# Attention stages of a four-layer decoder: output turned ahead of the weights, context keys ahead of the first turn, the addition and its norm one step later

## The chip, the cores and the metric

The kernel runs on one core of one Trainium2 chip. The time is that of the device, in microseconds (us), for one launch that does the whole decoder; lower is better. The core has five engines that run beside each other and meet at semaphores: TensorE (PE, with its weight loads PEld), VectorE (DVE), ScalarE (ACT), GpSimd (POOL) and SyncE (SP), which issues the transfers.

## What is computed

A decoder of four layers on 32 sequences of 64 tokens of 128 features, in float32. Each layer has a self-attention, an attention to a context and a feed-forward part, each with a residual addition. Six of the twelve parts go through the function that is changed. Cut to what matters, with one of the six written out:

```python
x = x + L0_attn(_layernorm(x), ...)                 # L0a: relative bias added to the scores
x = x + L1_xattn(_layernorm(x), ctx_1024, ...)      # L1x: plain softmax, keys and values of the context
x = x + L2_attn(_layernorm(x), ...)                 # L2a: low-rank maps, norms of queries and keys, causal
x = x + L3_attn(_layernorm(x), ...)                 # L3a: scores times a table of distances, causal
x = x + L3_xattn(_layernorm(x), ctx_1024, ...)      # L3x: sparsemax in place of softmax
x = x + L3_ffn(_layernorm(x), ...)                  # L3f: holds an attention (causal), then a gated part

def _L3_attn_ref(x, Wq, Wk, Wv, Wo, bo, rel_emb):
    q, k, v = heads(x @ Wq), heads(x @ Wk), heads(x @ Wv)        # 16 heads of 8
    scores = jnp.einsum('bhqd,bhkd->bhqk', q, k) * a_k
    scores = jnp.where(causal, -jnp.inf, scores)
    attn = jax.nn.softmax(scores / np.sqrt(hd), axis=-1)
    ctx = jnp.einsum('bhqk,bhkd->bhqd', attn, v)
    return merge(ctx) @ Wo + bo
```

## The kernel before, in words

The 2048 tokens are 16 tiles of 128 tokens (two sequences each), and four tiles make a quarter. A stage is one block with a program for each engine, written out in order; between stages all engines meet. Inside a stage the order of work is that in which the loops of `attention` (line 474) are written, and semaphores alone hold an engine back.

All engines run a loop over steps k of the same kind, one new tile a step, with later phases of earlier tiles behind it. `lag` is 1 in L0a and L3x and 2 in the others (line 527). On TensorE a step k is (lines 649 to 674): `scores(k)`, `turn_probs(k-lag)` (8 transposes of the weights), `turn_output(k-lag-2)` (a transpose of the normalised output), `weigh_values(k-lag-1)` (32 short matmuls in the trace, 16 in the program), `project(k-lag-2)`; in steps 1 and 2 of a quarter the keys and queries, and the values, of the quarter ahead follow. On VectorE a step k is (lines 940 to 955): `shift(k)` (two to four instructions over 128x1024), `normalise(k-lag-1)`, `add(k-lag-2)` of the projected tile to x, `measure` of the same tile, `scale(k-lag-3)`. ScalarE takes the transposed weights out of PSUM (two copies), then the transposed output, then makes the exponentials of tile k; in the sparse stage L3x the last (a Relu) comes first in the step. GpSimd spreads the keys of tile k over the heads (line 833) and inverts the variance for the norm of a later tile (line 842).

Outputs, turned outputs and projected tiles of tile t lie in PSUM bank 4 + t % 2 (lines 519 to 521). So `weigh_values(t)` may write only when `add(t-2)` has read the bank, and it waits for that:

```python
if t >= 2:
    pe.wait_ge(s.y_added, t - 1)
```

`scores(t)` waits until the scores of tile t-1 are read: after the first VectorE instruction of `shift` in L0a and L2a and L3f, after the second in L3a (semaphore `scored`), after the last in L1x (`shifted`). L3x computes all its scores ahead of the loop and runs twice, on 8 tiles each time; its VectorE step begins with `less_threshold(k)` in place of `shift(k)`. In L3f the addition goes to h and no norm follows inside the stage.

In the semaphore lists below, of stage L0a, signal_0_9 is `scores_ps`, 0_11 `scored`, 0_14 `probs_ready`, 0_15 `probsT_ps`, 0_16 `probsT_ready`, 0_17 `o_ps`, 0_19 `att_ready`, 0_21 `oT_ready`, 0_22 `y_ps` and 0_23 `y_added`.

Of the kernel before, what the change touches and what calls it, by code (L numbers as in the profile page):

```python
# [13 lines left out]
ACT = mybir.ActivationFunctionType  # L14
# [459 lines left out]
def attention(c, n, keys_from="h", mode="plain", q_scale=1.0, exp_scale=1.0, bias=False,  # L474
# [53 lines left out]
    with nc.Block() as block:  # L528
        @block.tensor
        def _(pe):  # L530
            def turn(q):
# [5 lines left out]
                    last = pe.transpose(c.ps[:, 6, tok(t % HT)], src[:, t], c.w("ident"))  # L537
                last.then_inc(s.turned_ps, 1)

            def keys_and_queries(q):  # L540
                pe.wait_ge(s.turned, q + 1)
                if q > 0:
                    pe.wait_ge(s.vx_ready, values_taken(q))
                pe.matmul(c.ps[:, 7], c.w(n + "_wk"), kvT[:, quarter(q)], start=True, stop=True).then_inc(s.k_ps, 1)
                pe.matmul(c.ps[:, 6], c.w(n + "_wq"), c.hT[:, quarter(q)], start=True, stop=True).then_inc(s.q_ps, 1)

            def values_of(t):
# [75 lines left out]
            def project(t):  # L623
                pe.wait_ge(s.oT_ready, t + 1)
                if out_bias:
                    pe.matmul(y_ps(t), c.w("ones")[0:1], c.w(n + "_bo")[0:1], start=True, stop=False)
                pe.matmul(y_ps(t), c.oT[:, tok(t)], c.w(n + "_wo"), start=not out_bias, stop=True)\
                    .then_inc(s.y_ps, 1)

            turn(0)  # L630
            if latent:
                for t in tiles_of(0):
# [16 lines left out]
            for k in range(nt + lag + 2):  # L649
                ahead, step = k // HT + 1, k % HT  # L650
                if not sparse:
                    if k < nt:
                        scores(k)
                    if k == 0 and not latent:
                        values(0)
                    if ahead < quarters and step == 0:
                        turn(ahead)
                if 0 <= k - lag < nt:
                    turn_probs(k - lag)
                if 0 <= k - lag - 2 < nt:  # L660
                    turn_output(k - lag - 2)
                if 0 <= k - lag - 1 < nt:
                    weigh_values(k - lag - 1)
                if 0 <= k - lag - 2 < nt:
                    project(k - lag - 2)
                if ahead < quarters and not sparse:
                    if latent and step < 2:
                        for t in range(HT * ahead + 2 * step, HT * ahead + 2 * step + 2):
                            latent_maps(t)
                    if latent and step == 3:  # L670
                        latent_turn(ahead)
                    if not latent and step == 1:
                        keys_and_queries(ahead)
                    if not latent and step == 2:
                        values(ahead)

        @block.scalar
        def _(act):
# [58 lines left out]
            def weights(k):  # L737
                if sparse:
                    act.wait_ge(sp.less_tau, k + 1)
                else:  # L740
                    act.wait_ge(s.shifted, k + 1)
                act.activation(buf(k), buf(k), ACT.Relu if sparse else ACT.Exp,  # L742
                               scale=exp_scale).then_inc(s.probs_ready, 1)

            take_turned(0)
            if latent:
                for t in tiles_of(0):
                    take_maps(t)
                take_roots(0)
                take_queries(0)  # L750
                take_keys(0)
            else:
                take_keys(0)
                take_queries(0)
            if sparse:
                for t in range(nt):
# [8 lines left out]

            for k in range(nt + lag + 2):
                ahead, step = k // HT + 1, k % HT
                if k < nt and sparse:
                    weights(k)
                if not sparse:  # L770
                    if k == 0 and not latent:
                        take_values(0)
                    if ahead < quarters and step == 0:
                        take_turned(ahead)
                t = k - lag
                if 0 <= t < nt:
                    for j in range(2):
                        act.wait_ge(s.probsT_ps, 2 * t + j + 1)
                        if t >= 2:

                            act.wait_ge(s.o_ps, t - 1)
                        act.copy(probsT(t)[:, j * 512:(j + 1) * 512], c.ps[:, 2 + j])\  # L782
                            .then_inc(s.probsT_ready, 1)
                t = k - lag - 2
                if 0 <= t < nt:
                    act.wait_ge(s.oT_ps, t + 1)
                    if bias:

                        act.activation(c.oT[:, tok(t)], oT_ps(t), ACT.Identity, bias=c.w(n + "_bv"))\
                            .then_inc(s.oT_ready, 1)  # L790
                    else:
                        act.copy(c.oT[:, tok(t)], oT_ps(t)).then_inc(s.oT_ready, 1)
                if k < nt and not sparse:
                    weights(k)
                if ahead < quarters and not sparse:
                    if latent and step < 2:
                        for t in range(HT * ahead + 2 * step, HT * ahead + 2 * step + 2):
                            take_maps(t)
                    if latent and step == 2:
                        take_roots(ahead)  # L800
                    if latent and step == 3:
                        take_queries(ahead)
                        take_keys(ahead)
                    if not latent and step == 1:
                        take_keys(ahead)
                        take_queries(ahead)
                    if not latent and step == 2:
                        take_values(ahead)

        @block.gpsimd  # L810
        def _(g):
            c.begin(g)
            if bias:
                g.tensor_scalar(c.scaled_bias[:], c.w(n + "_bq"), q_scale, None, ALU.mult)\
                    .then_inc(s.bias_scaled, 1)
            if rms:
                for q in range(2):
                    norm_gpsimd(c, g, r, 1e-6, q, "rms")
            if sparse:
                row_starts = c.room(6)[:, 0:nt * HEADS * TOP]  # L820
                g.memset(row_starts, 1.0).then_inc(sp.row_starts, 1)
                g.wait_ge(sp.row_starts, 1)
                g.memset(row_starts.rearrange("p (r k) -> p r k", k=TOP)[:, :, 0], 0.0)\
                    .then_inc(sp.row_starts, 1)

            def spread_keys(t):

                g.wait_ge(s.keys_ready, t + 1)
                if t >= 2:

                    g.wait_ge(s.scores_ps, t - 1)
                of_tile = c.room(2)[:, in_ring(t)].rearrange("p (b k) -> p b k", b=2)
                g.tensor_tensor(kx(t).rearrange("p (b h k) -> p b h k", b=2, k=S), bcast(of_tile, 2, HEADS // 2),  # L833
                                bcast(bcast(c.w("head_of_row"), 2, S), 1, 2), ALU.mult)\
                    .then_inc(s.kx_ready, 1)

            behind = nt if sparse else lag + 3
            for k in range(nt + behind):
                if k < nt:
                    spread_keys(k)  # L840
                if not rms and 0 <= k - behind < nt:
                    invert(c, g, following, k - behind)
                if rms and k % HT == 2 and k // HT + 2 < quarters:
                    norm_gpsimd(c, g, r, 1e-6, k // HT + 2, "rms")

        @block.vector
        def _(v):
# [89 lines left out]
                latent_norms(0)  # L937
            if sparse:
                thresholds(c, v, s, sp, buf)
            for k in range(nt + lag + 3):  # L940
                ahead, step = k // HT + 1, k % HT
                if k < nt:
                    if sparse:
                        less_threshold(k)
                    else:
                        shift(k)
                if 0 <= k - lag - 1 < nt:
                    normalise(k - lag - 1)
                if 0 <= k - lag - 2 < nt:
                    add(k - lag - 2)  # L950
                    if not rms:
                        v.wait_ge(s.y_added, k - lag - 1)
                        measure(v, following, c.x, k - lag - 2)
                if not rms and 0 <= k - lag - 3 < nt:
                    scale(v, following, c.x, c.h, k - lag - 3)
                if latent and ahead < quarters:
                    if step in (1, 2):
                        for t in range(HT * ahead + 2 * step - 2, HT * ahead + 2 * step):
                            latent_sums(t)
                    if step == 2:  # L960
                        latent_means(ahead)
                    if step == 3:
                        latent_norms(ahead)
                if rms and ahead + 1 < quarters:
                    if step == 2:
                        norm_measure(c, v, r, c.h, ahead + 1)
                    if step == 3:
                        norm_scale(c, v, r, c.h, c.hn, ahead + 1, "rms", c.w(n + "_n1"))
# [1409 lines left out]
```

## Time and profile before

| | |
|---|---|
| time, median of 3 runs | 2032.86 us (2019.84 to 2037.69) |
| profiled execution | 2030.96 us, its span 2029.1 us |
| mean granted TensorE clock of it | 0.762 of full |
| PE busy | 1271.8 us, 63% |
| DVE busy | 1104.3 us, 54% |
| POOL busy | 660.4 us, 33% |
| ACT busy | 556.2 us, 27% |

The changed function runs from about 125 to 229 us (L0a), 798 to 883 (L1x), 996 to 1160 (L2a), 1548 to 1669 (L3a), 1669 to 1867 (L3x, twice) and 1870 to 1979 (L3f). The rest of the span is other stages. A start of a step is best seen at the 128x1024 instructions of VectorE, which come once a tile. In a timeline an instruction's end is its start plus its duration; a number in square brackets is idle time of the engine just before, and the instruction that ended it.

### The profile page before, as it was taken

To read this page: it belongs to the slowest core of one execution; us is meant where nothing else is said; L and a number is where in the kernel's file an instruction comes from. 1 tells how busy PE (TensorE), PEld (TensorE's weight loads), DVE (VectorE), ACT (ScalarE), POOL (GpSimd) and SP (SyncE) were. 2 spreads that over 40 slices of the span, in tenths; PEclk is the share of its full clock that TensorE was granted. 3 is DMA by queue.
4 is the path that set the end of the run, shared out by engine and by line. 5 is a ranking of instruction groups with operands and counts; after the bars stand their busy time and mean duration, and the time that the engine had idled before them with its cause. 6 is when DMAs were issued, how large, how long until landed. Compare 5 with 4: busy or idle time off the path is not lost. (4 is left out here: it accounts for less than half of the span.)

```text
span 2029.1 us, 34354 instructions
## 1 busy us (share of the span) xinstructions
PE 1271.8 (63%) x13592; PEld 975.5 (48%) x13592; DVE 1104.3 (54%) x2991; ACT 556.2 (27%) x983; POOL 660.4 (33%) x697
## 2 busy tenths in 40 slices
PE   3049441883888886965366734338773874747797
PEld 3026341772677774644234524226661552525465
DVE  2039861114688885872467665612326965354673
ACT  0025210330122223621155211011112423332443
POOL 1015625332234443534222210542223322323321
PEclk7569655996899997967677665569996876655788
DMA  9970002552000000002000001024421000000000
GB/s 285 178 111 2 1 5 85 156 170 73 1 2 2 2 2 1 2 6 89 30 1 1 18 5 22 17 98 132 134 94 40 1 1 1 1 1 1 1 2 22
DMA packets 74052, 91.11 MB, mean 45 GB/s; under 512 B 5823, under 2 KB 61186, under 8 KB 73248
## 3 DMA queue, kind: packets, MB, share of 16 engines
q1 hardware_dynamic: 67872, 78.95, 15.7%
q0 software_dynamic: 6016, 9.93, 1.4%
q8 instruction: 108, 1.77, 0.3%
q14 instruction: 56, 0.46, 0.1%
HBM read 58.62 MB, written 32.69 MB: 45 GB/s over the span
## 5 line engine op out<-in xcount | busy, mean ns | idle before, releaser
L833 POOL TENSOR_TENSOR arena<-arena,small 128x1024 f32<-128x1024 f32 x96 | 184.4, 1927 | 160.8 <-ACT arena L691 98.5
L386 POOL TENSOR_SCALAR var_eps<-moments 128x1 f32<-128x1 f32 (+1 forms) x136 | 43.1, 317 | 415.3 <-DVE moments L379 415.3
L593 PE MATMUL ps<-arena,q 64*64 64x512 f32 x768 | 125.6, 727 | 59.8 <-issue 20.8
L742 ACT ACTIVATE arena<-arena 128x1024 f32<-128x1024 f32 x92 | 97.3, 1058 | 183.6 <-DVE arena L907 133.8
L603 PEld LDWEIGHTS ps<-small,arena 128*128 128x128 f32 x736 | 99.0, 164 | 81.4 <-ACT arena L742 47.0
L603 PE MATMUL ps<-small,arena 128*128 128x128 f32 x736 | 120.5, 317 | 24.5 <-ACT arena L742 22.7
L615 PE MATMUL ps<-vx,arena 128*64 128x18 f32 x3072 | 128.2, 230 | 0.7 <-DVE x L921 0.7
L615 PEld LDWEIGHTS ps<-vx,arena 128*64 128x64 f32 x3072 | 118.3, 162 | 20.9 <-issue 15.9
L1680 PEld LDWEIGHTS ps<-hT,L_qkv 128*128 128x128 f32 x1024 | 120.6, 197 | 14.2 <-DVE arena L1819 13.0
L1804 POOL TENSOR_TENSOR arena<-arena 128x1024 f32<-128x1024 f32 x32 | 75.4, 2357 | 158.2 <-DVE arena L1819 158.2
L1680 PE MATMUL ps<-hT,L_qkv 128*128 128x128 f32 x1024 | 125.4, 282 | 0.7 <-ACT hT L1765 0.7
L537 PE MATMUL ps<-small,h 128*128 128x128 f32 x80 | 17.7, 361 | 163.6 <-PEq L2217 97.8
L782 ACT COPY arena<-ps 128x512 f32<-128x512 f32 x192 | 104.2, 587 | 52.7 <-PE ps L603 52.0
L1350 PEld LDWEIGHTS ps<-expert_ring,arena 128*128 128x128 f32 (+1 forms) x864 | 105.2, 193 | 5.0 <-DVE arena L1572 1.9
L1331 PE MATMUL ps<-arena,expert_ring 128*112 128x256 f32 x368 | 86.4, 389 | 32.8 <-DVE arena L1572 30.2
L1350 PE MATMUL ps<-expert_ring,arena 128*128 128x128 f32 (+1 forms) x864 | 105.5, 276 | 1.7 <-DVE arena L1572 1.7
L388 POOL TENSOR_TENSOR rstd<-var_eps,minus_half 128x1 f32<-128x1 f32 (+1 forms) x136 | 94.9, 698 | 11.3
L537 PEld LDWEIGHTS ps<-small,h 128*128 128x128 f32 x80 | 11.5, 182 | 175.9 <-issue 175.4
L1586 DVE COPY arena<-ps 128x256 f32<-128x256 f32 x31 | 13.2, 425 | 142.2 <-PE ps L1350 142.2
L1331 PEld LDWEIGHTS ps<-arena,expert_ring 128*112 128x112 f32 x368 | 64.4, 180 | 50.9 <-issue 34.8
L1436 POOL DMA_INDIRECT home_L2f<-arena,home x46 | 44.8, 973 | 131.3 <-DVE arena L1586 102.9
L1339 PE MATMUL ps<-arena,expert_ring 128*128 128x256 f32 x248 | 66.4, 414 | 25.3 <-DMA expert_ring<-L0f_in 14.5
(324 smaller groups left out, 2811.0 us busy)
## 6 DMA issues: line engine op xcount, KB each, us to landing
expert_ring<-L2f_in SPq DMA_DIRECT2D x23, 704.0 KB, 4.3
expert_ring<-L0f_in SPq DMA_DIRECT2D x23, 578.0 KB, 3.9
slots_L0f<-blank SPq DMA_DIRECT2D x1, 8385.0 KB, 74.8
slots_L2f<-blank SPq DMA_DIRECT2D x1, 8385.0 KB, 58.4
small<-small_in SPq DMA_DIRECT2D x1, 4199.5 KB, 19.5
expert_ring<-L1f_in SPq DMA_DIRECT2D x8, 512.0 KB
arena<-slots_L0f SPq DMA_DIRECT2D x23, 129.0 KB, 3.2
arena<-slots_L2f SPq DMA_DIRECT2D x23, 129.0 KB
```

The lines of the kernel that those rows point to most:

```text
L388: g.tensor_tensor(m.rstd_of[:, own], m.var_eps_of[:, own], c.minus_half[:, 0:n], ALU.pow).then_inc(m.rstd, 1)
L593: last = pe.matmul(c.ps[part(b), m], c.q[part(m), at:at + S], kx(t)[part(m), b * 512:(b + 1) * 512], start=True, stop=True)
L603: last = pe.transpose(c.ps[:, 2 + k, j * P:(j + 1) * P], buf(t)[:, (4 * k + j) * P:(4 * k + j + 1) * P], c.w("ident"))
L615: last = pe.matmul(o_ps(t)[part(b), j * 18:(j + 1) * 18], probsT(t)[:, seq(j, b)], c.vx[:, t % 8, b, j], start=True, stop=True)
L742: act.activation(buf(k), buf(k), ACT.Relu if sparse else ACT.Exp, scale=exp_scale).then_inc(s.probs_ready, 1)
L782: act.copy(probsT(t)[:, j * 512:(j + 1) * 512], c.ps[:, 2 + j])\
L833: g.tensor_tensor(kx(t).rearrange("p (b h k) -> p b h k", b=2, k=S), bcast(of_tile, 2, HEADS // 2), bcast(bcast(c.w("head_of_row"), 2, S), ...
L1331: last = pe.matmul(c.ps[0:width, 2 * (m % 2) + k, cols], ring(j)[:, k * hid + i * width:k * hid + (i + 1) * width], xT(j), start=True, sto ...
L1339: last = pe.matmul(c.ps[:, m % 4, cols], ring(j)[:, i * P:(i + 1) * P], xT(j), start=True, stop=True)
L1350: last = pe.matmul(c.ps[:, 4 + j % 2, tok(b)], hidden(j)[:, i, tok(b)], ring(j)[0:width, down_at + i * D:down_at + (i + 1) * D], start=(i ...
L1680: last = pe.matmul(c.ps[:, pair(t, i) + m, (j % 4) * P:(j % 4 + 1) * P], w[:, at:at + P], c.hT[:, tok(t)], start=True, stop=True)
L1804: g.tensor_tensor(rotated[i], rotated[i], sines[i], ALU.add).then_inc(signal, 1)
```

## The change

In `attention`, on all engines:

- TensorE: `turn_output(k-lag-2)` goes ahead of `turn_probs(k-lag)`. Where the keys come from the context (L1x, L3x) the keys of quarter 0 are projected ahead of the first turn.
- ScalarE: the copy of the turned output goes ahead of the two copies of the turned weights; the context keys are taken first; in L3x the Relu of tile k goes to the end of the step.
- VectorE: `add` handles tile k-lag-3 in step k instead of k-lag-2, and stands between `shift(k)` and `normalise(k-lag-1)`; `measure` (same tile as `add`) stays behind `normalise`, `scale` handles k-lag-4. The loop is one step longer.
- GpSimd: the inversion comes one step later.

No instruction is added or removed, and no wait is changed. The diff, cut to its core:

```diff
             def keys_and_queries(q):
                 pe.wait_ge(s.turned, q + 1)
                 if q > 0:
                     pe.wait_ge(s.vx_ready, values_taken(q))
-                pe.matmul(c.ps[:, 7], c.w(n + "_wk"), kvT[:, quarter(q)], start=True, stop=True).then_inc(s.k_ps, 1)
+                if q > 0 or keys_from == "h":
+                    project_keys(q)
...
+            if keys_from == "ctx":
+                project_keys(0)
             turn(0)
...
+                if 0 <= k - lag - 2 < nt:
+                    turn_output(k - lag - 2)
                 if 0 <= k - lag < nt:
                     turn_probs(k - lag)
-                if 0 <= k - lag - 2 < nt:
-                    turn_output(k - lag - 2)
                 if 0 <= k - lag - 1 < nt:
                     weigh_values(k - lag - 1)
...
-                if k < nt and sparse:
-                    weights(k)
...
+                t = k - lag - 2
+                if 0 <= t < nt:
+                    act.wait_ge(s.oT_ps, t + 1)
...
+                        act.copy(c.oT[:, tok(t)], oT_ps(t)).then_inc(s.oT_ready, 1)
                 t = k - lag
...
-                if k < nt and not sparse:
+                if k < nt:
                     weights(k)
...
-            behind = nt if sparse else lag + 3
+            behind = nt if sparse else lag + 4
...
-            for k in range(nt + lag + 3):
+            for k in range(nt + lag + 4):
                 ahead, step = k // HT + 1, k % HT
                 if k < nt:
                     if sparse:
                         less_threshold(k)
                     else:
                         shift(k)
+                if 0 <= k - lag - 3 < nt:
+                    add(k - lag - 3)
                 if 0 <= k - lag - 1 < nt:
                     normalise(k - lag - 1)
-                if 0 <= k - lag - 2 < nt:
-                    add(k - lag - 2)
-                    if not rms:
-                        v.wait_ge(s.y_added, k - lag - 1)
-                        measure(v, following, c.x, k - lag - 2)
                 if not rms and 0 <= k - lag - 3 < nt:
-                    scale(v, following, c.x, c.h, k - lag - 3)
+                    v.wait_ge(s.y_added, k - lag - 2)
+                    measure(v, following, c.x, k - lag - 3)
+                if not rms and 0 <= k - lag - 4 < nt:
+                    scale(v, following, c.x, c.h, k - lag - 4)
```

The first place is TensorE in L0a, from the scores of one tile (L593, now L597) to the projection (L626/L627, now L630/L631). Before:

```order
L593 MATMUL ps<-arena,q 64x512 [waits signal_0_11,signal_0_8,signal_0_5]
L593 MATMUL ps<-arena,q 64x512 x3
L603 MATMUL ps<-small,arena 128x128 [waits signal_0_16,signal_0_14]
L603 MATMUL ps<-small,arena 128x128 x3
L603 MATMUL ps<-small,arena 128x128 [waits signal_0_16]
L603 MATMUL ps<-small,arena 128x128 x3
L621 MATMUL ps<-small,att 128x128 [waits signal_0_19]
L615 MATMUL ps<-vx,arena 64x18 [waits signal_0_16,signal_0_7,signal_0_23]
L615 MATMUL ps<-vx,arena 64x18 x15
L626 MATMUL ps<-small 128x128 [waits signal_0_21]
```

And now:

```order
L597 MATMUL ps<-arena,q 64x512 [waits signal_0_11,signal_0_8,signal_0_5]
L597 MATMUL ps<-arena,q 64x512 x3
L625 MATMUL ps<-small,att 128x128 [waits signal_0_19]
L607 MATMUL ps<-small,arena 128x128 [waits signal_0_16,signal_0_14]
L607 MATMUL ps<-small,arena 128x128 x3
L607 MATMUL ps<-small,arena 128x128 [waits signal_0_16]
L607 MATMUL ps<-small,arena 128x128 x3
L619 MATMUL ps<-vx,arena 64x18 [waits signal_0_16,signal_0_7,signal_0_23]
L619 MATMUL ps<-vx,arena 64x18 x15
L630 MATMUL ps<-small 128x128 [waits signal_0_21]
```

The transpose of the output (L621, now L625) has moved ahead of the eight transposes of the weights (L603, now L607); the weighing (L615, now L619) waits for `y_added` (signal_0_23) as it did.

The second place is VectorE in L0a, one step from the first instruction of `shift` to the scaling. Before:

```order
L894 TENSOR_TENSOR arena<-ps,bias 128x1024 [waits signal_0_9,signal_0_15]
L905 TENSOR_REDUCE row_max<-arena 128x16 [waits signal_0_11]
L907 TENSOR_TENSOR arena<-arena,row_max 128x1024 [waits signal_0_12]
L913 RECIPROCAL row_inv<-ps 128x16 [waits signal_0_17]
L915 TENSOR_TENSOR att<-ps,row_inv 128x128 [waits signal_0_18]
L921 TENSOR_TENSOR x<-x,ps 128x128 [waits signal_0_22]
L376 BN_STATS stats<-x 128x6 [waits signal_0_23]
L379 BN_AGGR moments<-stats 128x2 [waits signal_0_25]
L395 TENSOR_SCALAR h<-x,moments,rstd 128x128 [waits signal_0_28]
```

And now:

```order
L901 TENSOR_TENSOR arena<-ps,bias 128x1024 [waits signal_0_9,signal_0_15]
L912 TENSOR_REDUCE row_max<-arena 128x16 [waits signal_0_11]
L914 TENSOR_TENSOR arena<-arena,row_max 128x1024 [waits signal_0_12]
L928 TENSOR_TENSOR x<-x,ps 128x128 [waits signal_0_22]
L920 RECIPROCAL row_inv<-ps 128x16 [waits signal_0_17]
L922 TENSOR_TENSOR att<-ps,row_inv 128x128 [waits signal_0_18]
L376 BN_STATS stats<-x 128x6 [waits signal_0_23]
L379 BN_AGGR moments<-stats 128x2 [waits signal_0_25]
L395 TENSOR_SCALAR h<-x,moments,rstd 128x128 [waits signal_0_28]
```

The addition (L921, now L928) has moved from behind the normalising (L913 and L915, now L920 and L922) to ahead of it, and is that of the tile before.

The third place is ScalarE in the first part of L3x, the steps of its last two tiles (these two lie in the expert ring). L742 (now L748) is the Relu, L782 (now L798) the two copies of the turned weights, L789 (now L787) the turned output. Before:

```order
L742 ACTIVATE expert_ring<-expert_ring 128x1024 [waits signal_1_42]
L782 COPY arena<-ps 128x512 [waits signal_1_17,signal_1_15] x2
L789 ACTIVATE oT<-ps,small 128x128 [waits signal_1_20]
L742 ACTIVATE expert_ring<-expert_ring 128x1024 [waits signal_1_42]
L782 COPY arena<-ps 128x512 [waits signal_1_17,signal_1_15] x2
L789 ACTIVATE oT<-ps,small 128x128 [waits signal_1_20]
```

And now:

```order
L748 ACTIVATE expert_ring<-expert_ring 128x1024 [waits signal_1_42]
L787 ACTIVATE oT<-ps,small 128x128 [waits signal_1_20]
L798 COPY arena<-ps 128x512 [waits signal_1_17,signal_1_15] x2
L748 ACTIVATE expert_ring<-expert_ring 128x1024 [waits signal_1_42]
L787 ACTIVATE oT<-ps,small 128x128 [waits signal_1_20]
L798 COPY arena<-ps 128x512 [waits signal_1_17,signal_1_15] x2
```

The order within a step was Relu, weights, output, and is now output, weights, Relu.

## Rows read from the trace of the kernel before

**Rows 1.** Page, part 1: busy us (share of the span) x instructions.

```profile
PE 1271.8 (63%) x13592; PEld 975.5 (48%) x13592; DVE 1104.3 (54%) x2991; ACT 556.2 (27%) x983; POOL 660.4 (33%) x697
```

**Rows 2.** Windows: columns from:to, us, engines busy, PEclk, DMA, GB/s; L0a, L1x, L3a, L3x, L3f.

```profile
130.00:213.00 83.00, 73.00 (x914) 47.67 (x913) 74.05 (x121) 45.80 (x76) 39.55 (x40) 0.96 0.02 5
798.00:871.00 73.00, 67.97 (x841) 42.80 (x840) 53.34 (x99) 43.85 (x75) 38.87 (x38) 0.93 0.01 2
1556.00:1651.00 95.00, 77.24 (x854) 50.19 (x848) 91.20 (x131) 42.17 (x73) 36.89 (x37) 0.89 0.00 1
1716.00:1766.00 50.00, 37.00 (x360) 31.32 (x360) 21.81 (x57) 18.82 (x32) 9.71 (x16) 0.60 0.00 1
1878.00:1967.00 89.00, 72.60 (x849) 47.31 (x845) 70.86 (x110) 42.47 (x73) 30.05 (x23) 0.83 0.00 1
```

**Rows 3.** Timeline, DVE, L0a: start us, us, instruction [idle before <-releaser].

```profile
204.77 1.22 DVE L894 TENSOR_TENSOR arena<-ps,bias 128x1024 f32<-128x1024 f32 x1
...
208.47 0.24 DVE L913 RECIPROCAL row_inv<-ps 128x16 f32<-128x16 f32 x1
...
208.95 0.28 DVE L921 TENSOR_TENSOR x<-x,ps 128x128 f32<-128x128 f32 x1
...
209.92 1.22 DVE L894 TENSOR_TENSOR arena<-ps,bias 128x1024 f32<-128x1024 f32 x1
```

**Rows 4.** Timeline, PE, same step of L0a.

```profile
205.67 1.11 PE L615 MATMUL ps<-vx,arena 128*64 128x18 f32 x32
206.71 0.48 PE L626 MATMUL ps<-small 1*128 1x128 f32 x2
207.13 0.49 PE L627 MATMUL ps<-small,oT 128*128 128x128 f32 x2
207.56 1.09 PE L593 MATMUL ps<-arena,q 64*64 64x512 f32 x8
```

**Rows 5.** Timeline, all engines, L0a where DVE waits for scores.

```profile
182.01 1.02 PE L545 MATMUL ps<-hT,small 128*128 128x512 f32 x2
...
182.96 1.09 PE L593 MATMUL ps<-arena,q 64*64 64x512 f32 x8
...
184.19 1.23 DVE L894 TENSOR_TENSOR arena<-ps,bias 128x1024 f32<-128x1024 f32 x1 [0.48 <-PE ps L593]
```

**Rows 6.** Timeline, all engines, last tiles of L0a.

```profile
216.91 1.90 PE L615 MATMUL ps<-vx,arena 128*64 128x18 f32 x32
...
218.74 0.79 PE L626 MATMUL ps<-small 1*128 1x128 f32 x2
...
219.46 0.80 PE L627 MATMUL ps<-small,oT 128*128 128x128 f32 x2
...
220.05 0.42 PE L621 MATMUL ps<-small,att 128*128 128x128 f32 x1
220.30 0.29 DVE L921 TENSOR_TENSOR x<-x,ps 128x128 f32<-128x128 f32 x1 [0.85 <-PE ps L627]
...
220.64 0.62 PE L615 MATMUL ps<-vx,arena 128*64 128x18 f32 x8 [0.17 <-DVE x L921]
```

**Rows 7.** Timeline, all engines, L2a, scores after an idle stretch.

```profile
1124.81 1.99 PE L593 MATMUL ps<-arena,q 64*64 64x512 f32 x8 [2.75 <-issue]
...
1126.93 1.23 DVE L900 TENSOR_TENSOR arena<-ps,small 128x1024 f32<-128x1024 f32 x1 [6.03 <-PE ps L593]
```

**Rows 8.** Timeline, all engines, one step of L3x, first part.

```profile
1735.76 1.22 DVE L925 TENSOR_TENSOR arena<-arena,row_inv 128x1024 f32<-128x1024 f32 x1
...
1738.91 0.38 ACT L789 ACTIVATE oT<-ps,small 128x128 f32<-128x128 f32 x1
...
1739.35 0.79 PE L626 MATMUL ps<-small 1*128 1x128 f32 x2 [0.86 <-ACT oT L789]
...
1740.90 0.29 DVE L921 TENSOR_TENSOR x<-x,ps 128x128 f32<-128x128 f32 x1 [1.78 <-PE ps L627]
...
1741.88 1.22 DVE L925 TENSOR_TENSOR expert_ring<-expert_ring,row_inv 128x1024 f32<-128x1024 f32 x1
```

More of the change, by code:

```diff
@@ L538, in turn, with project_keys @@
                 last.then_inc(s.turned_ps, 1)
+            def project_keys(q):
+                pe.matmul(c.ps[:, 7], c.w(n + "_wk"), kvT[:, quarter(q)], start=True, stop=True).then_inc(s.k_ps, 1)
             def keys_and_queries(q):
@@ L743, in weights @@
                                scale=exp_scale).then_inc(s.probs_ready, 1)
+            if keys_from == "ctx":
+                take_keys(0)
             take_turned(0)
@@ L752, in _ @@
             else:
-                take_keys(0)
+                if keys_from == "h":
+                    take_keys(0)
                 take_queries(0)
@@ L774, in _ @@
                         take_turned(ahead)
+                t = k - lag - 2
+                if 0 <= t < nt:
+                    act.wait_ge(s.oT_ps, t + 1)
+                    if bias:
+                        act.activation(c.oT[:, tok(t)], oT_ps(t), ACT.Identity, bias=c.w(n + "_bv"))\
+                            .then_inc(s.oT_ready, 1)
+                    else:
+                        act.copy(c.oT[:, tok(t)], oT_ps(t)).then_inc(s.oT_ready, 1)
                 t = k - lag
@@ L783, in _ @@
                             .then_inc(s.probsT_ready, 1)
[L784 to L792, printed above, removed]
-                if k < nt and not sparse:
+                if k < nt:
                     weights(k)
```

## The prediction

> **What bounds the kernel now.** I read the page first [rows 1]: no engine is full over the span, so the stages have to be read one by one. The windows of the attention stages [rows 2] show VectorE at 74.05 of 83 us in L0a and 91.20 of 95 in L3a, with TensorE's clock near full; L3x stands apart, with VectorE at 21.81 of 50 us and the clock at 0.60. Then the timelines. In L0a a step runs from 204.77 to 209.92, 5.15 us, and VectorE works through it without a gap [rows 3]. Of it 3.70 are `shift` (three wide instructions, to 208.47) and 1.45 the rest. TensorE is ahead: the weighing starts at 205.67, the projection's two matmuls at 206.71 and 207.13, the next scores at 207.56 [rows 4], so the weighed tile waits for VectorE, not the reverse. In L3x the step is a chain through three engines [rows 8]: threshold at 1735.76, the turned output copied at 1738.91 behind the Relu and two copies, projection at 1739.35, addition at 1740.90 after 1.78 us of idle VectorE, next threshold at 1741.88: 6.12 us.
>
> **What the change does to the steps with `shift`.** The addition of tile k-lag-3 now follows `shift(k)`. `weigh_values(k-lag-1)` waits for exactly that addition, since the two tiles share a bank. Before, that addition was a step back and the wait was met long before. Now TensorE, which could begin at 205.67, must wait for an addition that starts at 208.47. Behind it in TensorE's order stand the projection and `scores(k+1)`, and VectorE's next `shift` waits for those scores; VectorE itself waits for the weighing before it can normalise. So what ran beside each other becomes one loop: scores, shift, add, weigh, project, scores.
>
> Its price in L0a at the full clock: shift 3.70 [rows 3]; start of the addition to start of the weighing 220.30 to 220.64, 0.34 [rows 6]; weighing 1.04, bias matmul 0.42, output matmul 0.43 [rows 4]; start of the scores to start of the next shift 182.96 to 184.19, 1.23 [rows 5]. Sum 7.16 against 5.15: +2.0 a step. VectorE's own way (3.70 + 0.34 + the weighing's 1.11 and a hand-over of 0.05 + 1.45 less the addition's 0.28) is 6.4 and lies inside.
>
> The same at half clock: weighing 1.83, bias 0.72, output 0.59 [rows 6], scores to shift 2.12 [rows 7]: 3.70 + 0.34 + 1.83 + 0.72 + 0.59 + 2.12 = 9.30, +4.15 a step.
>
> The other modes follow from these rows. A wide instruction takes 1.25 (3.70 over three). L2a has L0a's VectorE work (5.15) and no bias matmul: 6.74 or 8.58, +1.6 or +3.4. L3a has one wide instruction more (6.40): 8.41 or 10.55, +2.0 or +4.15. L1x has one less (3.9) and no bias: 5.49 or 7.33, +1.6 or +3.4. L3f is L2a without measuring and scaling (4.4): 6.74 or 8.58, +2.3 or +4.2.
>
> Addition and shift stand in one step from k = lag+3 to 15: 12 steps in L0a, 11 in the others. That gives
>
> - full clock: L0a 24, L1x 17, L2a 17.5, L3a 22, L3f 25: 106 us;
> - half clock: 50, 37, 37.5, 45.5, 46: 216 us.
>
> **Keys, queries and values of the quarter ahead** stand on TensorE between the projection and the next scores, so they now lie on the loop in two quarters of each of L0a, L1x, L3a and L3f. Keys and queries are 2 x 0.95 [rows 5], the values 16 short matmuls, about one weighing, 1.04 (an estimate): 2.9 a quarter. Part is paid already (0.48 in rows 5, more in L1x, where scores wait for the last shift). I take 1.5 a quarter at full clock, 12 us in all, and 30 at half.
>
> **Which clock.** The level decides half of the sum. TensorE's work in a step of L0a is about 4.0 us at the full level: 1.04 + 0.42 + 0.43 and 1.02 for the scores [rows 4], and the nine transposes at 1.1 (an estimate: what 73.00 us of busy time for 16 tiles [rows 2] leaves, less keys and values), 78% of 5.15, and the granted clock is 0.96 [rows 2]. In the new loop it is 56% in L0a, 55% in L2a and L3f, 48% in L3a, 67% in L1x, with an idle stretch of 2 to 4 us between the transposes and the weighing. The nearest rows are L3x's: some 3 us of work in 6.12, idle in pieces of no more than 2 us, clock 0.60; and L3a's: 4.0 in 6.40, clock 0.89. So I put L0a, L2a and L3f 60% of the way to half clock, L3a 70%, L1x 25%: 40 + 22 + 30 + 39 + 37 = 168, and the extras 22. Together +190. [...]
>
> **L3x gains.** ScalarE now hands over the turned output first and the Relu last, and VectorE adds a tile whose projection was done a step ago. The chain of 6.12 breaks up. VectorE's loop is threshold 1.14, addition to weighing 0.34, weighing to normalising 1.16, and 1.17 behind: 3.8 at full clock. TensorE's busy time bounds it otherwise: 37.0 us for 8 tiles at clock 0.60 [rows 2], 4.6 a tile. The steps also contain some shorter than 6.12 (50 us for 8 tiles and the drain). Over 7 steps and two parts: -28 us at full clock, -8 at half, I take -18.
>
> **The rest.** Turning the output first costs nothing: its input was normalised a step earlier, and 0.2 us of TensorE is moved into idle time. The early context keys start the keys sooner, but the queries still wait for the turn, and scores need both; -1 us over three starts. The inversion on GpSimd moves with the measuring, and the spreading of keys behind it keeps its distance; one more loop step in the drain is hidden by a drain already shorter than the chain in it.
>
> **Sum** against the profiled execution of 2030.96 us (1.90 below the median of the runs): 2031 + 190 - 18 - 1 = **2202 us**, +8.4%.
>
> **Rivals.**
>
> - *The clock stays at full.* For it: L3a holds 0.89 with 64% work. Against: L3x at 0.60. 2031 + 118 - 28 = 2121. Chance 0.14.
> - *Half clock nearly throughout.* For it: the idle stretch comes in every step, and the weighing behind it is a row of very short matmuls. Against: after it come 3 to 4 us of dense work. 2031 + 246 - 8 = 2269. Chance 0.12.
> - *The bank wait does not bind, and the kernel is faster.* If TensorE came to the weighing later than the addition, the loop would not close, and L3x's 28 us would be all: 2003, 1.4% faster. The place is the start of L615, 205.67; the point from which it decides is 208.8, the end of an addition that starts at 208.47, so TensorE would have to be 3.1 us later than it is in every step. Nothing in the rows delays it; chance 0.03.
> - *The change does what it says but moves nothing*, because the gain of L3x and a loop half as costly cancel: this would need a loop of only +0.4 a step; 2031. Chance 0.03.
>
> My forecast, the mixed clock, has 0.68, from about 2140 to 2255. With the two clock rivals' nearer halves the range is 2118 to 2262. A measurement of this kernel can't tell less than 1% (20 us) from no change; faster by more 0.03, within 0.03, slower by more 0.94.
>
> **What would show it.** TensorE's L619 would stand idle before it with the addition (L928) as its releaser, some 2 to 4 us a step, and VectorE's normalising (L920) idle behind the weighing and its first shift instruction behind the scores. L0a's steps would be 7.2 to 9.3 us, L1x's 5.5 to 7.3. In L3x steps below 5 us and no idle before the addition. The granted clock in L0a well below 0.96. I am wrong if L619 does not wait for L928, or if the steps lengthen by less than the 2.0 of the full clock.

## The result and the profile after

| | before | changed |
|---|---|---|
| time, median of 4 runs | 2031.71 us (2019.84 to 2037.69) | 2245.26 us (2231.86 to 2247.11) |
| span of the profiled execution | 2029.1 us | 2244.8 us |
| mean granted TensorE clock | 0.762 | 0.717 |

The changed kernel takes 1.1036 times the time of the kernel before (95% interval 1.0992 to 1.1080). The forecast was 2202 us in a range of 2118 to 2262. The way and the mechanism of the loop were right, the gain in L3x did not come, and the size was 43 us short.

The page of the changed kernel, busy time by engine:

```profile
PE 1387.9 (62%) x13592; PEld 1045.0 (47%) x13592; DVE 1105.3 (49%) x2991; ACT 570.4 (25%) x983; POOL 659.2 (29%) x697
```

Against [rows 1] VectorE does the same work, 1105.3 us. TensorE has the same 13592 instructions and is busy 116 us longer, which is the lower clock. The other 100 us are idle time. The windows say where the clock fell, in the order L0a, L1x, L2a, L3a, L3x, L3f (columns as in [rows 2]: engines PE, PEld, DVE, ACT, POOL, then PEclk):

```profile
133.00:262.00 129.00, 98.13 (x878) 61.83 (x877) 74.35 (x118) 48.05 (x77) 38.66 (x38) 0.72 0.01 2
850.00:940.00 90.00, 71.54 (x811) 44.14 (x810) 53.14 (x95) 44.04 (x73) 35.35 (x35) 0.87 0.01 2
1094.00:1260.00 166.00, 106.33 (x857) 64.64 (x849) 94.89 (x196) 66.65 (x125) 36.36 (x37) 0.66 0.00 1
1669.00:1815.00 146.00, 98.09 (x842) 63.60 (x840) 92.47 (x128) 46.10 (x74) 37.23 (x35) 0.69 0.00 1
1886.00:1936.00 50.00, 42.52 (x360) 36.50 (x360) 20.61 (x57) 20.09 (x32) 8.87 (x16) 0.50 0.01 1
2049.00:2178.00 129.00, 89.37 (x804) 56.22 (x800) 72.23 (x107) 44.47 (x73) 29.74 (x22) 0.70 0.00 1
```

In L0a VectorE's 74 us of work now take 129 us in place of 83; in L3a 92 us take 146 in place of 95. VectorE was the bound there and is now idle for a third of the time and more. The clock went from 0.96 to 0.72 and from 0.89 to 0.69, and L3x, which was at 0.60, is at 0.50.

What L619, the weighing, waited for over the whole changed kernel, and who waited for it (us in all, times):

```profile
its engine sat idle before it (us, times) until:
  DVE x L928: 241.4, 102
  DVE h L928: 55.6, 23
...
who waited for it (us, times):
  DVE row_inv L920: 181.5, 87
```

TensorE stood 297 us behind the addition, with the addition of the kernel before 4.1 us (3.9 to x and 0.2 to h); VectorE's normalising stood 181.5 us behind the weighing (53.5 before). One step of L0a, timeline of all engines, shows the loop whole, and answers to [rows 3, 4]:

```profile
231.30 1.23 DVE L901 TENSOR_TENSOR arena<-ps,bias 128x1024 f32<-128x1024 f32 x1 [2.14 <-PE ps L597]
...
234.96 0.28 DVE L928 TENSOR_TENSOR x<-x,ps 128x128 f32<-128x128 f32 x1
...
235.29 1.90 PE L619 MATMUL ps<-vx,arena 128*64 128x18 f32 x32 [2.02 <-DVE x L928]
...
237.12 0.79 PE L630 MATMUL ps<-small 1*128 1x128 f32 x2
237.24 0.26 DVE L920 RECIPROCAL row_inv<-ps 128x16 f32<-128x16 f32 x1 [2.00 <-PE ps L619]
...
237.85 0.80 PE L631 MATMUL ps<-small,oT 128*128 128x128 f32 x2
...
238.57 1.99 PE L597 MATMUL ps<-arena,q 64*64 64x512 f32 x8
...
240.69 1.23 DVE L901 TENSOR_TENSOR arena<-ps,bias 128x1024 f32<-128x1024 f32 x1 [2.22 <-PE ps L597]
```

Shift to 234.96, addition, weighing at 235.29, projection at 237.12 and 237.85, scores at 238.57, next shift at 240.69: no two of them lie beside each other. The step is 9.39 us; the sum for half clock was 9.30, and the same step took 5.15 before.

Taken from the starts of the 16 additions of each stage (both timelines), first to last, against the terms of the prediction, the quarter extras spread over their four stages:

| stage | before | after | first to last | shift of the last addition within the stage | predicted |
|---|---|---|---|---|---|
| L0a | 75.1 | 118.4 | +43.3 | +47.6 | +45.5 |
| L1x | 56.2 | 82.3 | +26.1 | +25.8 | +27.5 |
| L2a | 101.7 | 133.0 | +31.3 | +36.2 | +30 |
| L3a | 86.0 | 134.0 | +48.0 | +54.4 | +44.5 |
| L3x | 2 x 34.8 | 2 x 31.7 | -6.1 | +3.4 | -18 |
| L3f | 71.8 | 110.9 | +39.1 | +46.1 | +42.5 |

The column before the last also holds the later first addition of each stage; with 2.9 us that the profiled execution had lost before L0a began, it sums to 216.3 us.

### The profile page after: what moved, and what is told of

The parts are those of the page before. It is cut to its first block and busy times, and to the rows that moved or that the text cites. A ratio compares the mean times of both kernels' runs of the same rounds, so it can differ in the third digit from the quotient of the medians.

```text
span 2244.8 us, 34354 instructions
## 1 busy us (share of the span) xinstructions
PE 1387.9 (62%) x13592; PEld 1045.0 (47%) x13592; DVE 1105.3 (49%) x2991; ACT 570.4 (25%) x983; POOL 659.2 (29%) x697
## 5 line engine op out<-in xcount | busy, mean ns | idle before, releaser
L619 PE MATMUL ps<-vx,arena 128*64 128x18 f32 x3072 | 151.1, 248 | 139.3 <-DVE x L928 113.2
L619 PEld LDWEIGHTS ps<-vx,arena 128*64 128x64 f32 x3072 | 140.8, 188 | 167.1 <-DVE x L928 128.2
L386 POOL TENSOR_SCALAR var_eps<-moments 128x1 f32<-128x1 f32 (+1 forms) x136 | 43.3, 319 | 568.5 <-DVE moments L379 568.3
L597 PE MATMUL ps<-arena,q 64*64 64x512 f32 x768 | 154.4, 886 | 47.6 <-issue 17.2
L607 PE MATMUL ps<-small,arena 128*128 128x128 f32 x736 | 137.8, 350 | 19.5 <-ACT arena L748 17.9
L607 PEld LDWEIGHTS ps<-small,arena 128*128 128x128 f32 x736 | 123.0, 189 | 29.7 <-ACT arena L748 22.4
L748 ACT ACTIVATE arena<-arena 128x1024 f32<-128x1024 f32 x92 | 97.3, 1058 | 140.1 <-DVE arena L914 110.1
L798 ACT COPY arena<-ps 128x512 f32<-128x512 f32 x192 | 107.9, 589 | 52.7 <-PE ps L607 51.9
L920 DVE RECIPROCAL row_inv<-ps 128x16 f32<-128x16 f32 x96 | 24.7, 257 | 181.5 <-PE ps L619 181.5
L901 DVE TENSOR_TENSOR arena<-ps,bias 128x1024 f32<-128x1024 f32 x16 | 19.6, 1224 | 144.3 <-PE ps L597 144.3
L1338 PEld LDWEIGHTS ps<-arena,expert_ring 128*112 128x112 f32 x368 | 64.2, 179 | 51.1 <-issue 34.8
L907 DVE TENSOR_TENSOR arena<-ps,small 128x1024 f32<-128x1024 f32 x32 | 39.2, 1224 | 99.0 <-PE ps L597 99.0
```

The lines of the kernel that those rows point to most:

```text
L386: g.tensor_scalar(m.var_eps_of[:, own], m.moments_of[:, own, 1], 1e-5, None, ALU.add).then_inc(m.var_eps, 1)
L597: last = pe.matmul(c.ps[part(b), m], c.q[part(m), at:at + S], kx(t)[part(m), b * 512:(b + 1) * 512], start=True, stop=True)
L607: last = pe.transpose(c.ps[:, 2 + k, j * P:(j + 1) * P], buf(t)[:, (4 * k + j) * P:(4 * k + j + 1) * P], c.w("ident"))
L619: last = pe.matmul(o_ps(t)[part(b), j * 18:(j + 1) * 18], probsT(t)[:, seq(j, b)], c.vx[:, t % 8, b, j], start=True, stop=True)
L1338: last = pe.matmul(c.ps[0:width, 2 * (m % 2) + k, cols], ring(j)[:, k * hid + i * width:k * hid + (i + 1) * width], xT(j), start=True, sto ...
```

## The experiments

The first question is whether the place of the addition is all of it. In the kernel **add_back** only VectorE's loop and the inversion are put back; TensorE's and ScalarE's new orders and the early keys stay.

```diff
-                if 0 <= k - lag - 3 < nt:
-                    add(k - lag - 3)
                 if 0 <= k - lag - 1 < nt:
                     normalise(k - lag - 1)
+                if 0 <= k - lag - 2 < nt:
+                    add(k - lag - 2)
...
```

> The changed kernel with only VectorE's (and the inversion's) loop put back: add of tile k-lag-2 behind normalise; output turned first, ScalarE's order and the early context keys stay. My theory (the addition behind shift closes a loop of scores, shift, add, weigh, project, and that is all of the loss): 2015 to 2035 us, L0a steps of 5.15, no idle of TensorE before the weighing but in the drain. Rival (turning the output first and the new order on ScalarE cost by themselves): above 2080. In L3x I expect steps of 5.2 to 6.1, TensorE at half clock.

Measured: 2032.34 us, 1.0021 times the kernel before (0.9993 to 1.0048). The wait is gone:

```profile
  DVE x L928: 3.0, 9
  DVE h L928: 0.2, 1
```

**only_add** is the opposite: the kernel before with VectorE's loop and the inversion alone.

> The kernel before with only VectorE's loop (and the inversion) changed, nothing else. My theory: all of the loss, 2235 to 2255 us, and L0a steps of 8 to 10 as in the changed kernel. Rival (the loss needs the other moves too): below 2180.

Measured: 2222.14 us, 1.0997 (1.0914 to 1.1079). That is 13 us below the range that I expected, but far from the rival's 2180, and its weighing (L615 there) waits as long as in the full change:

```profile
  DVE x L921: 239.1, 104
  DVE h L921: 56.7, 22
```

So the one moved block makes the loss: put back it returns 213 us, alone it costs 194. To the full change 23 us are missing; about 13 of them lie in L3x, whose two parts run 92.7 and 94.0 us from last addition to last addition here and 100.1 and 99.1 in the full change (96.6 and 99.2 in the kernel before). So in L3x VectorE's new order alone gains 9 us, and the full change loses 3. The intervals of the two ratios overlap, so the 23 us themselves are not clear of the noise.

The block was moved in two ways at once: the addition is of an older tile, and it stands behind `shift`. **add_first** keeps the older tile and puts it ahead.

```diff
+                if 0 <= k - lag - 3 < nt:
+                    add(k - lag - 3)
                 if k < nt:
                     if sparse:
                         less_threshold(k)
                     else:
                         shift(k)
-                if 0 <= k - lag - 3 < nt:
-                    add(k - lag - 3)
```

> The changed kernel with the addition of tile k-lag-3 ahead of shift(k) instead of behind it, still one step later than before. My theory (the cost is that the bank is freed only after shift, not that it is freed a step later): 2010 to 2040 us, L0a steps of 5.15 to 5.2, no idle before the weighing. Rival (a bank pair with the addition a step later is one bank too few wherever it stands): 2150 or more.

Measured: 2033.32 us, 1.0032 (0.9997 to 1.0067). The weighing waits for the addition 5.7 us in all, and VectorE's L0a steps are again without a gap, 4.99 us each:

```profile
202.54 1.22 DVE L901 TENSOR_TENSOR arena<-ps,bias 128x1024 f32<-128x1024 f32 x1
...
207.33 0.28 DVE L928 TENSOR_TENSOR x<-x,ps 128x128 f32<-128x128 f32 x1
207.53 1.22 DVE L901 TENSOR_TENSOR arena<-ps,bias 128x1024 f32<-128x1024 f32 x1
```

An addition one step late costs nothing that these runs can tell; an addition behind 3.7 us of `shift`, while TensorE waits for its bank, costs nearly all of the loss.

**filler** asks what the lower clock is worth. It is the changed kernel with matmuls whose result nobody reads, in the idle stretch ahead of the weighing, in the last four steps with `shift` of each stage. One matmul of 512 columns in L1x, two in the others.

```diff
                 if 0 <= k - lag < nt:
                     turn_probs(k - lag)
+                if not sparse and nt - HT <= k < nt:
+                    pe.wait_ge(s.q_ready, nt)
+                    for _ in range(1 if mode == "plain" else 2):
+                        pe.matmul(c.ps[:, 6], c.w("ident"), c.hT[:, quarter(0)], start=True, stop=True)
```

> The changed kernel with matmuls of 512 columns whose result nobody reads put on TensorE ahead of the weighing in the last four steps with a shift of L0a, L1x (one) and L2a, L3a, L3f (two), where it idles. Theory (part of the loss is the half clock that the idle stretch brings): these steps fall to the full-clock sums, 7.2 in L0a, 5.5 in L1x, 6.7 in L2a and L3f, 8.4 in L3a, from 8.3 to 10.7 now; about 2215 to 2235 us in all. Rival (the clock falls all the same, or the idle is not what lowers it): steps the same or longer by up to the filler's 1.9 us each, 2245 to 2270.

Measured: 2197.02 us, 1.083 (1.0775 to 1.0886): 48 us less than the changed kernel, with more work, and below the 2215 to 2235 that I expected. Two steps of L2a (L932 is the addition, L671 the added matmuls):

```profile
1228.71 1.11 PE L619 MATMUL ps<-vx,arena 128*64 128x18 f32 x32 [1.28 <-DVE x L932]
...
1231.40 1.23 DVE L911 TENSOR_TENSOR arena<-ps,small 128x1024 f32<-128x1024 f32 x1 [0.29 <-PE ps L597]
...
1232.23 1.88 PE L671 MATMUL ps<-hT,small 128*128 128x512 f32 x4
...
1235.39 1.11 PE L619 MATMUL ps<-vx,arena 128*64 128x18 f32 x32 [1.28 <-DVE x L932]
```

The weighing takes 1.11 us, its time at the full level [rows 4], where the step of L0a above shows 1.90. The step is 6.68 us, three times over; the sum for full clock was 6.74. In L1x it is 5.42 (sum 5.49), and one of L3a's is 8.36 (sum 8.41). In the changed kernel the same steps were 7.9 to 8.7 us in L2a and 10.66 at the end of L3a. The loop itself, with TensorE's wait of 1.28 us behind the addition, stays. Not all of the 48 us come from the added matmuls. Between the two profiled executions lie 43 us, and 9 of them are in L3x, where none was added: in the second half of each of its parts the clock was 0.85 and 0.84 here and 0.50 in the changed kernel. The other 34 lie in and ahead of the five stages that have the added matmuls.

**keys_first** is the kernel before with the early context keys alone.

> The kernel before with only the early context keys of L1x and L3x. My theory (the queries still wait for the turn, and scores need both): 0 to -2 us on 2030, within the noise. Rival (the first scores come sooner by the whole projection): -2 us in each of three starts, -6.

Measured: 2034.27 us, 0.9998 (0.9969 to 1.0027): nothing, as the sum had it. The rival's -6 us lies just inside the interval, so the time does not exclude it. The trace speaks against it: counted from the last addition before, the first additions of L3x's two parts come after 64.3 and 63.1 us, and came after 61.9 and 64.4.

The other runs are on L3x, where 18 us were expected and none came. **sparse_only** is the kernel before with the new orders of TensorE, ScalarE and VectorE in L3x alone.

> The kernel before, with the new order of all engines in the sparse stage L3x alone (without the early keys); the other stages keep the old order. Theory from the changed kernel's trace (L3x becomes TensorE-bound at half clock, 5.20 us a step in place of 5.5 to 6.1, and its first addition comes a step later): -2 to -8 us on 2030. Rival (my prediction's own sum for L3x): -18 or more.

Measured: 2026.60 us, 0.9969 (0.9946 to 0.9992), as the theory had it. A window of its loop in the first part:

```profile
1725.00:1755.00 30.00, 29.48 (x304) 26.00 (x304) 12.76 (x38) 14.30 (x24) 6.49 (x10) 0.60 0.00 1
```

TensorE is busy 29.48 of 30 us and is granted 0.60. The chain through three engines is gone, and here TensorE at a low clock has taken its place. The second part went otherwise. From the first to the fifth addition of either part the windows are:

```profile
1730.48:1750.49 20.01, 20.01 (x184) 17.70 (x184) 8.58 (x28) 10.14 (x17) 4.97 (x7) 0.54 0.01 2
1824.76:1840.16 15.40, 13.32 (x184) 11.50 (x184) 8.57 (x27) 9.83 (x17) 4.96 (x7) 0.92 0.01 1
```

The same loop ran at 0.54 in one part and at 0.92 in the other of one execution. The first steps are 5.6, 5.5 and 5.2 us in the first part, and 5.2, 3.8 and 3.8 in the second. What decides between them no run shows. **sparse_fill** adds one matmul of 512 columns to each step of that kernel, on the engine that bounds it, and **sparse_fill_t** eight transposes instead.

```diff
                 if 0 <= k - lag < nt:
                     turn_probs(k - lag)
+                if sparse and k < nt:
+                    pe.matmul(c.ps[:, 0], c.w("ident"), c.hT[:, quarter(0)], start=True, stop=True)
```

> As sparse_only, with one matmul of 512 columns that nobody reads put on TensorE in every step of L3x that has a threshold. Theory (what keeps the clock at half in L3x is the kind of work, short matmuls and transposes, not idle time: the 512-column matmul raises it): granted clock of the steps at 0.8 or more, steps of 3.8 to 4.2 after the first two or three, -15 to -25 us on 2030. Rival (TensorE is full already and the clock does not rise): 5.2 + 1.9 = 7.1 us a step, +20 to +30 us.

> As sparse_fill, with eight transposes of 128 columns in place of the one matmul of 512, about the same time on TensorE. If the kind of instruction decides (transposes of 128 do not raise the clock): clock at 0.5, steps of about 7.0, +20 to +30 us on 2030. Rival (any denser work raises it): as sparse_fill, -15 to -25.

Measured: 2010.68 us, 0.9891 (0.9864 to 0.9918) and 2018.35 us, 0.9926 (0.9892 to 0.9959). Windows of the loop, first of sparse_fill (one in each part), then of sparse_fill_t:

```profile
1722.00:1736.00 14.00, 13.31 (x162) 9.90 (x158) 8.06 (x20) 8.46 (x15) 2.83 (x4) 1.00 0.00 1
1818.00:1830.00 12.00, 12.00 (x149) 8.97 (x149) 7.44 (x22) 7.75 (x14) 5.45 (x8) 1.00 0.01 1
```

```profile
1727.00:1740.00 13.00, 12.31 (x193) 11.16 (x193) 5.79 (x13) 8.63 (x14) 1.67 (x2) 1.00 0.00 1
```

More work on the engine that was the bound made its loop shorter: the first three steps are 3.8 to 4.2 us in all four parts, where sparse_only had 5.2 to 5.6 in its first part and reached 3.8 in its second only from the second step on. So the added work does not give a level that the loop never had: in these executions it had it from the first step, in both parts. My theory that the kind of instruction decides, with transposes counting for nothing, fell with sparse_fill_t; the rival, that any further dense work does it, held for the two kinds tried. sparse_fill is the best version of the case, 1.1% faster than the kernel before. How small the addition may be was not tried.

Last, which of L3x's new orders matters. **sparse_add_b** is the kernel before with VectorE's new order in L3x only, the Relu still first on ScalarE, and **sparse_add_fill_b** the same with the added matmul.

> The kernel before, with only VectorE's addition (and what follows it) one step later and ahead of the normalising in L3x; ScalarE keeps the Relu first, TensorE its order. Theory (the new order on ScalarE holds back the second tile's Relu, since the copies of the first tile's weights stand ahead of it, and costs some 3 to 5 us at each start of L3x): -8 to -14 us on 2031, L3x 92 to 94 us from the last addition of one part to that of the next. Rival (ScalarE's order is free): as sparse_only, 2022 to 2027.

> As sparse_add_b, with the matmul of 512 columns that nobody reads in every step of L3x that has a threshold. Theory (both gains add up): 2000 to 2009 us, steps of 3.8 to 4.2 and L3x 84 to 88 us a part. Rival (with the Relu first the projection comes late, and the steps stay near 5): 2010 to 2020.

Measured: 2024.10 us, 0.9974 (0.9954 to 0.9994) and 2022.62 us, 0.9962 (0.9949 to 0.9975). The first had 5 us where 8 to 14 were expected, no more than sparse_only within the intervals; its two parts, 92.7 and 91.9 us, are as the theory had them, but sparse_only's, 94.6 and 90.2, sum to the same, so the time decides little. The trace settles where the start is lost: the first addition comes 12.65 and 13.71 us after the first threshold here, and 16.15 in both parts of sparse_only. The second missed both its ranges, and the two gains do not add. Its steps swing between 3.4 and 6.6 us and its parts are 98.4 and 94.7 us, longer than without the matmul, although the clock from first to fifth addition is 0.84 and 0.91. The projection comes late, and VectorE waits for it:

```profile
1752.52 0.29 DVE L923 TENSOR_TENSOR x<-x,ps 128x128 f32<-128x128 f32 x1 [0.67 <-PE ps L627]
```

So the added matmul pays in sparse_fill (0.9891) and not here. The two differ in ScalarE's order and in TensorE's, since here the added matmul stands ahead of the turned output; which of the two matters, no run parts.

## Why the prediction was right, and where its sizes were off

**The loop.** Right, and shown three ways: by its rows, by add_back and only_add, and by add_first, which leaves all as it is except that the addition is not behind `shift`. The two sums for a step, 7.16 and 9.30 us in L0a and their kin, were worked out from rows of separate places and came within 0.1 us of steps that ran at one level throughout (9.39; 6.68, 5.42 and 8.36). Not every step of filler did: L3a's other two took 9.04 and 9.26, and L0a's lie between 7.09 and 7.75. Two shares of work in the prediction are a little off by its own numbers, 53% in place of 55 in L2a and L3f and 65% in place of 67 in L1x; no term hangs on them.

**The clock.** Its share was the open quantity, and in the sum it came out as I took it: from first to last addition the five stages with the loop are 187.8 us longer, against 190 predicted (L3a 3.5 over, L3f 3.4 under, the others within 2.2). Part of this is luck. L2a was summed from steps of 5.15 us, which only its last three steps with a `shift` had before; its others took 6.04 us or more, and its steps grew by 2.0 to 4.9 us, where 1.6 to 3.4 was forecast. The rival by which the clock stays full fell, with 0.72 in L0a's window. There a weighing at 158.64 us took 1.11 us, the full level, and the scores of the same step, at 161.13, took 1.99, the half level; TensorE's longest idle stretch in that window is 3.00 us, before a weighing. The Trainium skill (TensorE: Matmul & The Clock Gate, Part 1 and the closing table) names idle time of TensorE as what lowers the clock. L0a's rows, with an idle stretch in every step, agree in kind; those of L3x below do not. What the level is worth can be read from filler: with it raised in the last four steps and the drains some 34 us.

**The later first addition, a term put at nothing.** A stage's first addition comes later by 4.3 us in L0a, 4.9 in L2a, 6.4 in L3a and 7.0 in L3f; in L1x it does not (-0.3). The prediction's part on the rest put the extra loop step at nothing. It is not: the first additions wait behind a `shift` too. Together these are 22 us that stand in none of the terms, and they, not the steps, are about half of the 43 us. In add_first, which has the extra step too but the addition ahead of `shift`, the first additions of L2a, L3a and L3f come only 1.3 to 1.8 us later.

**L3x, the mis-sized term.** Predicted -18, measured +3.4: these 21 us are the other half of what the forecast fell short. 12 of them are the loop, which gave 6.1 us in place of 18, and 9 are the starts of the two parts, for which the prediction has no term. The step that failed in the loop is the clock at which it would run: I took 3.8 us at full and 4.6 at the 0.60 of [rows 2], both of which need the clock to hold or rise once the gaps are gone. The 3.8 itself was right for full clock: sparse_only's second part has steps of 3.77 and 3.78. One step of the changed kernel, TensorE alone:

```profile
1912.24 0.42 PE L625 MATMUL ps<-small,att 128*128 128x128 f32 x1
1912.45 1.92 PE L607 MATMUL ps<-small,arena 128*128 128x128 f32 x8
1914.30 1.90 PE L619 MATMUL ps<-vx,arena 128*64 128x18 f32 x32
1916.13 0.79 PE L630 MATMUL ps<-small 1*128 1x128 f32 x2
1916.85 0.80 PE L631 MATMUL ps<-small,oT 128*128 128x128 f32 x2
1917.44 0.42 PE L625 MATMUL ps<-small,att 128*128 128x128 f32 x1
```

There is no gap, as forecast no idle time stands before the addition, and the step is 5.20 us in place of 6.12. But every duration is that of the half level, and the steps below 5 us that were named as a sign came only once before the drain (5.60, 5.45, 5.21, 4.35 and 5.20). The window says it of several steps:

```profile
1896.00:1918.00 22.00, 21.42 (x183) 19.03 (x184) 9.92 (x26) 10.10 (x17) 3.88 (x6) 0.50 0.01 1
```

The chain broke up and gave 3.0 us a part (34.75 to 31.72 us, first to last addition). The start took them back. The first addition comes 16.14 us after the first threshold, 12.65 before (16.15 and 13.70 in the second part). Of this 2.2 us is a threshold that comes later, because the second Relu stands behind the copies in ScalarE's new order and TensorE waits for it:

```profile
1888.49 1.97 PE L607 MATMUL ps<-small,arena 128*128 128x128 f32 x8 [6.81 <-ACT arena L748]
...
1890.98 1.06 ACT L748 ACTIVATE arena<-arena 128x1024 f32<-128x1024 f32 x1
1892.10 1.97 PE L607 MATMUL ps<-small,arena 128*128 128x128 f32 x8 [1.63 <-ACT arena L748]
```

Before, the two Relus ran as one row and the 16 transposes without a stop. The experiments put this cost on the new orders of ScalarE and TensorE, and not on the late addition: the first addition comes 15.96 and 15.95 us after the first threshold in add_back, which has these two orders without VectorE's, 16.15 twice in sparse_only, which lacks the early keys, and 12.72 and 11.91 in only_add, which has VectorE's alone. From first threshold to last addition the parts are 47.86 and 47.87 us, and were 47.40 and 48.45. What is left, 3.0 us in the first part and 0.5 in the second, lies ahead of the first threshold, and no run tells why.

**The rest.** The early keys are worth nothing (keys_first), and the new orders of TensorE and ScalarE gain nothing with VectorE's old order (add_back, 1.0021).

## What to carry to other kernels

Before a consumer is moved on an in-order engine, look at who waits for the buffer that it frees: behind a long instruction, a small read can turn a ring of two banks into one serial loop. The price of such a loop can be summed from the starts and durations of its links at both clock levels, and the spread between the two is the real uncertainty. Where TensorE is the bound at half clock, look at the granted clock before taking work off it; here a matmul too many made one loop faster and, in another order of the engines, did not.

## What the runs showed of the hardware

- A TensorE without gaps is not a TensorE at full clock: busy 21.42 of 22 us in L3x of the changed kernel, granted 0.50. Of a step of 5.20 us there, 1.90 are the weighing, matmuls of 18 columns. The Trainium skill (TensorE: Matmul & The Clock Gate, Part 1) puts a low clock down to idle time, and these rows do not agree.
- Nor is the level of such a loop fixed: in one execution of sparse_only the same loop was granted 0.54 in its first part, busy 20.01 of 20.01 us, and 0.92 in its second, busy 13.32 of 15.40.
- One matmul of 512 columns more a step (1.02 us), or eight transposes, and the loop ran at 1.00 in both parts of the profiled execution. The same page of the Trainium skill (Part 4) says that the full level does not engage for transposes; in sparse_fill_t the added work was transposes alone, and these rows do not agree.
- A mean such as the 0.72 of L0a hides steps of both levels: distances of its additions run from 7.09 us (sum for full clock 7.16) over 9.39 (sum for half 9.30) to 11.62 where the quarter ahead is projected.
